# Combine weights from DRAM rows instead of a one-hot matmul, the output projection inside the expert loop, and half of the gating moved into it

## The reference, cut to what matters

```python
xn = _layernorm(x)                       # layer 0 before this: differential attention, MXFP4 ffn
s  = attn(xn) @ Wo + bo                  # 16 heads of 16
w, idx = _gate(xt, gate_w)               # top 4 of 16 experts, weights sum to 1
combine = einsum('tk,tke->te', w, one_hot(idx))
h1 = einsum('td,eid->tei', xt, W1); h3 = einsum('td,eid->tei', xt, W3)
g  = silu(h1) * h3 * combine[:, :, None]
y  = einsum('tei,edi->td', g, W2)
z  = silu(xt @ Ws1.T) * (xt @ Ws3.T) @ Ws2.T
x  = x + s * silu(y + z)
```

## Time and profile before

| | us |
|---|---|
| median of 3 runs | 946.36 |
| profiled execution, its own time | 948.34 |
| its span in the profile | 946.6 |
| start of `experts` (first instruction behind the barrier) | 672.5 |
| unit 2 begins on PE | 706.8 |
| last matmul of `down` ends | 933.9 |

### The profile page before, as it was taken

How to read it: one execution, slowest core, us unless ns; L and a number is a source line. 1 busy time by engine, 2 the same in 40 slices (tenths; PEclk the granted TensorE clock), 3 DMA queues, 4 the chain that set the end, 5 groups by cost and what they waited for, 6 DMA issues and landing times. The chain is left out here.

```text
span 946.6 us, 12914 instructions
## 1 busy us (share of the span) xinstructions
PE 791.8 (84%) x3682; PEld 386.6 (41%) x3682; DVE 508.8 (54%) x1448; ACT 424.5 (45%) x925; POOL 411.4 (43%) x753
## 2 busy tenths in 40 slices
PE   3848999889889998853695989788479999999995
PEld 2322333323323322223461223222257777777774
DVE  3748777767666765014428768672024444444445
ACT  2422555545545654511131457567314444444442
POOL 0831676425333242212221222342337677777774
PEclk9965999999999999955986799899779999999998
DMA  5485331100110110120076462232100000000001
GB/s 167 150 267 117 80 85 29 44 19 14 42 35 13 42 30 18 28 72 10 0 213 188 127 174 68 73 120 75 56 12 0 0 0 1 0 1 0 0 0 45
DMA packets 52206, 57.09 MB, mean 60 GB/s; under 512 B 13338, under 2 KB 39291, under 8 KB 52142
## 3 DMA queue, kind: packets, MB, share of 16 engines
q1 hardware_dynamic: 52148, 56.42, 21.3%
HBM read 34.70 MB, written 15.40 MB: 53 GB/s over the span
## 5 line engine op out<-in xcount | busy, mean ns | idle before, releaser
L660 ACT ACTIVATE top<-ps 128x512 f32<-128x512 f32 (+3 forms) x384 | 161.3, 497 | 156.5 <-PE ps L608 152.5
L591 PE MATMUL ps<-mid 96*128 96x512 bf16 (+3 forms) x576 | 192.3, 362 | 27.0 <-PEq L230 11.5
L608 PE MATMUL ps<-mid 99*128 99x512 bf16 (+3 forms) x576 | 182.4, 340 | 28.1 <-DMA mid<-top 9.5
L694 DVE CUSTOM_DVE_ANT_0 ps<-ps,keep 128x512 f32<-128x512 f32 (+3 forms) x384 | 183.9, 503 | 28.6 <-PE ps L591 27.4
L1374 PE MATMUL ps<-xp,wp 128*128 128x512 f32 (+1 forms) x600 | 146.9, 394 | 8.3 <-POOL wp L1467 8.3
L628 PE MATMUL ps<-top,mid 128*33 128x512 f32 (+3 forms) x768 | 150.5, 515 | 0.4 <-ACT top L660 0.4
L1374 PEld LDWEIGHTS ps<-xp,wp 128*128 128x128 f32 (+1 forms) x600 | 113.4, 189 | 34.1 <-issue 9.2
L777 POOL TENSOR_SCALAR_AFFINE_SELECT top<-top 128x128 f32<-128x128 f32 x256 | 72.4, 302 | 115.5 <-ACT top L660 110.7
L608 PEld LDWEIGHTS ps<-mid 99*128 99x128 bf16 x576 | 56.0, 100 | 152.6 <-issue 59.5
L698 DVE TENSOR_REDUCE top<-ps 128x1 f32<-128x512 f32 x128 | 88.0, 688 | 49.6 <-PE ps L591 49.6
L660 ACT ACTIVATE mid<-ps 128x512 f32<-128x512 f32 (+1 forms) x192 | 81.5, 493 | 62.2 <-PE ps L608 60.0
(11 more groups left out here) (201 smaller groups left out, 835.2 us busy)
## 6 DMA issues: line engine op xcount, KB each, us to landing
mid<-part_scratch SPq DMA_DIRECT2D x9, 1152.0 KB, 8.9
part_scratch<-top SPq DMA_DIRECT2D x18, 384.0 KB, 5.0
top<-in_w SPq DMA_DIRECT2D x16, 396.0 KB, 4.0
part_scratch<-top SPq DMA_DIRECT2D x18, 256.0 KB, 5.0
top<-inverse_scratch SPq DMA_DIRECT2D x16, 256.0 KB
mid<-part_scratch SPq DMA_DIRECT2D x9, 384.0 KB, 3.9
top<-in_w SPq DMA_DIRECT2D x8, 384.0 KB, 5.5
part_scratch<-top SPq DMA_DIRECT2D x18, 128.0 KB, 5.9
```

What stands on the lines that cost most here:

```text
L591: nc.tensor.matmul(ps[:, s_bank(turn), 0:w], queries(pair, m)[0:PARTS, i * P:(i + 1) * P], keys(pair, m)[0:PARTS, c * 512:c * 512 + w], st ...
L608: nc.tensor.matmul(ps[:, ST_BANK + n % AHEAD, 0:w], keys(pair, m)[0:STACK, j * P:(j + 1) * P], queries(pair, m)[0:STACK, q0:q0 + w], start ...
L660: nc.scalar.activation(pr[:, n % RING, 0:w], ps[:, ST_BANK + n % AHEAD, 0:w], ACT.Exp, scale=0.25).then_inc(p_ready, 1)
L694: ins = nc.vector.tensor_tensor_reduce(bank, bank, msk[:, 512 - w:512], -1.0 if low else 1.0, 3e38 if low else -3e38, ALU.add, ALU.min if ...
```

## The change

In `middle`, the combine weights stay float32: the split into three parts goes, PE transposes them in float32, ACT copies them to a tile `rows17`, and SP writes this to a DRAM tensor `combine_rows` (17 rows of 1024) at the stage's end. The first fetches of rows in layer 1 attention wait for that write.

In `experts`, the matmul L1382, its table and its bank go. For each unit SP issues two DMAs that read one 2 KB row each of `combine_rows` and repeat it over the partitions of that expert, into one of two tiles `cw`; `g` reads `cw` in place of PSUM. From unit 2 on, SP waits for `g` of two units before. The projection moves: token tiles 0 to 3 behind `down` of unit 3's step, tiles 4, 5 and 6, 7 in the steps of tiles 22 and 23 of the first half, into two banks, and DVE's additions of `bo` go to steps 3 and 24. PE's first matmuls wait only for the parts that they read. The first four tiles are transposed, gated and stored at the end of the loop (PE in the last two steps, ACT and DVE behind their last unit's work), and only tiles 4 to 7 behind `down`; the copy of `yT` is shared by ACT and DVE.

```diff
@@ middle, sync
+                sp.wait_ge(cT_ok, NC)
+                sp.dma_start(comb, rows17).then_inc(env["comb_kept"], 16)
@@ middle, scalar
-                    nc.scalar.copy(combT[:, c, :], psb[0:51, 2, c * 512:(c + 1) * 512]).then_inc(cT_ok, 1)
+                    nc.scalar.copy(rows17[:, c * 512:(c + 1) * 512], ps[0:E + 1, 2 + c, :]).then_inc(cT_ok, 1)
@@ middle, vector
-                        link(nc.vector.memset(cb[:, :, E:E + 1], 0.5))
-                        link(nc.vector.tensor_copy(cp[:, :, 0, :], cb[:, :, :]))
-                        link(nc.vector.tensor_tensor(cr[:, :, :], cb[:, :, :], cp[:, :, 0, :], ALU.subtract))
-                        link(nc.vector.tensor_copy(cp[:, :, 1, :], cr[:, :, :]))
-                        nc.vector.tensor_tensor(cp[:, :, 2, :], cr[:, :, :], cp[:, :, 1, :], ALU.subtract).then_inc(cb_ok, 1)
+                        nc.vector.memset(cb[:, :, E:E + 1], 0.5).then_inc(cb_ok, 1)
@@ experts, sync
+                def combine_weights(n):
+                    c, i = divmod(n, GI)
+                    if n >= 2:
+                        sp.wait_ge(g_ok, n - 1)
...
+                    for lo, hi in ((0, cut), (cut, r)):
+                        e = min((i * P + lo) // I, E)
+                        sp.dma_start(cw[lo:hi, n % 2, :], comb[e:e + 1, c * 512:(c + 1) * 512].to_broadcast([hi - lo, 512])
+                                     ).then_inc(cw_ok[n % 2], 16)
+                combine_weights(0)
+                combine_weights(1)
                 sp.dma_start(wo1[:, :, :], env["wo1"].rearrange("(c p) n -> p c n", p=P)).then_inc(ld, 16)
                 sp.dma_start(bo[:, :], env["bo"].partition_broadcast(P)).then_inc(ld, 16)
-                sp.dma_start(ones[:, :], env["onehot"]).then_inc(ld, 16)
                 env["last_inverses"](sp)
+                for n in range(2, UNITS):
+                    combine_weights(n)
@@ experts, tensor
+                            if begin and bank == H1 and j == 1:
+                                pe.wait_ge(xl_ok, 1)
+                            if begin and bank == H1 and j == 2:
+                                pe.wait_ge(wl_ok, 1)
...
-                    if isinstance(n, int) and n == 0:
-                        through_wo()
-                        pe.wait_ge(s1_ok, 4)
-                    nc.tensor.matmul(ps[0:r, CB + b, :], ones[:, bass.ds(i * P, r)], combT[:, c, :],
-                                     start=True, stop=True).then_inc(c_ok, 1)
...
+                    if c == 0 and isinstance(i, int) and 3 <= i < 4:
+                        for q in range(2):
+                            through_wo(q)
+                    if c == 0 and isinstance(i, int) and i >= GI - 3 and i < GI - 1:
+                        through_wo(2 + i - (GI - 3))
+                    if c == 1 and isinstance(i, int) and i >= GI - 2:
+                        if i == GI - 2:
+                            pe.wait_ge(s1_ok, 4)
+                        for t in range(2):
+                            back(2 * (i - (GI - 2)) + t, SB_ + i - (GI - 2), t * D)
@@ experts, vector
-                    dve.wait_ge(c_ok, n + 1)
+                    dve.wait_ge(cw_ok[b], cw_turn(c, k, i))
...
-                    nc.vector.tensor_tensor(g[0:r, b, :], a3[0:r, b, :], ps[0:r, CB + b, :],
-                                            ALU.mult).then_inc(g_ok, 1)
+                    nc.vector.tensor_tensor(g[0:r, b, :], a3[0:r, b, :], cw[0:r, b, :], ALU.mult).then_inc(g_ok, 1)
+                    if c == 0 and isinstance(i, int) and i in (3, GI - 1):
+                        for q in range(2):
+                            summed(q if i == 3 else 2 + q)
+                    if c == 1 and isinstance(i, int) and i == GI - 1:
+                        gates(0)
                 sweep(nc.vector.Fori, step)
+                gates(1)
+                dve.wait_ge(y_ok, UNITS)
+                nc.vector.tensor_copy(yT[:, 1, 1, :], ps[:, YB + 1, :]).then_inc(yTd_ok, 1)
```

More of the change, by code:

```diff
@@ L143, in program @@
         st6o = sb("st6o", [P, 4, 2, 6], F32, high)
[L144 to L145 removed]
+        comb = nc.dram_tensor("combine_rows", [E + 1, T], F32, kind="Internal").ap()
+        row_stats, comb_kept = sem("row_stats"), sem("comb_kept")
         v0 = sb("v0", [P, 4, NT, 33], F32, mid)
@@ L1297, in experts @@
         bo = new("bo_s", [P, D], F32)
-        ones = new("onehot_s", [51, NI], BF16)
+        cw = new("cw_s", [P, 2, 512], F32)
         s1 = new("s1", [P, NT, D], F32)
@@ L1327, in sweep, with tiles, pairs @@
                     step(c, i, i)
+        def tiles(q):
+            return slice(2 * q, 2 * q + 2)
+        def pairs(v):
+            return v.rearrange("p (t d) -> p t d", t=2)
         def slot(c, k):
@@ L1343, in _ @@
+                for q in range(2):
+                    sp.wait_ge(fo_ok, q + 1)
+                    sp.dma_start(out[2 * q * P:2 * (q + 1) * P, :].rearrange("(t p) d -> p t d", p=P),
+                                 gg[:, tiles(q), :]).then_inc(stored, 16)
+                for t in range(4, NT):
+                    sp.wait_ge(fo_ok, t - 1)
                     sp.dma_start(out[t * P:(t + 1) * P, :], gg[:, t, :]).then_inc(stored, 16)
-                sp.wait_ge(stored, 16 * NT)
+                sp.wait_ge(stored, 16 * (2 + 4))
@@ L1346, in _ @@
             @block.tensor
             def _(pe):
[L1349 to L1359, removed]
@@ L1361, in _, with through_wo @@
-                pe.wait_ge(xl_ok, 1)
+                def through_wo(q):
+                    if q == 0:
+                        pe.wait_ge(ld, 32)
+                        pe.wait_ge(env["combined1"], NC * 2)
+                    if q >= 2:
+                        pe.wait_ge(s1_ok, q - 1)
+                    for t in (2 * q, 2 * q + 1):
+                        for k in range(KD):
+                            last = nc.tensor.matmul(ps[:, SB_ + q % 2, (t % 2) * D:(t % 2 + 1) * D],
+                                                    o1[:, k, t * P:(t + 1) * P],
+                                                    wo1[:, k, :], start=k == 0, stop=k == KD - 1)
+                    last.then_inc(s_mm, 1)
@@ L1363, in hidden, with back @@
+                def back(t, bank, at):
+                    for k in range(KD):
+                        last = nc.tensor.transpose(ps[:, bank, at + k * P:at + (k + 1) * P],
+                                                   yT[:, t // 4, k, (t % 4) * P:(t % 4 + 1) * P], idf[:, :])
+                    last.then_inc(z_ok, 1)
                 def hidden(c, k, i):
                     n, b, r = c * GI + i, slot(c, k), rows(i)
+                    begin = isinstance(n, int) and n == 0
                     if isinstance(n, int) and n == GI:
@@ L1367, in hidden @@
                         pe.wait_ge(xl2_ok, 1)
-                    pe.wait_ge(wl_ok, n + 1)
+                    if begin:
+                        pe.wait_ge(xh_ok, 1)
+                        pe.wait_ge(wh_ok, 1)
+                    else:
+                        pe.wait_ge(wl_ok, n + 1)
                     if not (isinstance(n, int) and n < 2):
@@ L1409, in _ @@
                     down(NC - 1, i, i)
-                for t in range(NT):
-                    c = t // 4
-                    pe.wait_ge(yT_ok, c + 1)
-                    for k in range(KD):
-                        last = nc.tensor.transpose(ps[:, t, k * P:(k + 1) * P],
-                                                   yT[:, c, k, (t % 4) * P:(t % 4 + 1) * P], idf[:, :])
-                    last.then_inc(z_ok, 1)
+                pe.wait_ge(yT_ok, 2)
+                pe.wait_ge(yTd_ok, 1)
+                for t in range(4, NT):
+                    back(t, H1 + t - 4, 0)
             @block.scalar
             def _(act):
-                act.wait_ge(ld_m, 16 * 25)
                 def high_w13(b, i):
@@ L1431, in _, with gates @@
                 nc.scalar.copy(xp[:, 0, :, 512:T], xT[:, :, 512:T]).then_inc(xh_ok, 1)
+                def gates(q):
+                    act.wait_ge(z_ok, 2 * q + 2)
+                    nc.scalar.activation(ty[:, q, :], ps[:, SB_ + q, :], ACT.Tanh, scale=0.5).then_inc(ty_ok, 1)
                 def step(c, k, i):
@@ L1489, in _, with residual @@
                 sweep(nc.gpsimd.Fori, step)
-                for t in range(NT):
-                    pool.wait_ge(gated, t + 1)
-                    nc.gpsimd.tensor_tensor(gg[:, t, :], gg[:, t, :], xs[:, t, :], ALU.add).then_inc(fo_ok, 1)
+                def residual(part, done):
+                    pool.wait_ge(gg_ok, done)
+                    nc.gpsimd.tensor_tensor(gg[:, part, :], gg[:, part, :], xs[:, part, :], ALU.add).then_inc(fo_ok, 1)
+                for q in range(2):
+                    residual(tiles(q), 2 * q + 2)
+                for t in range(4, NT):
+                    residual(slice(t, t + 1), 4 + 2 * (t - 4) + 2)
             @block.vector
```

91 lines of the change are left out of this document (55 added, 36 removed).

## The result

The changed kernel takes 914.29 us (median of 4 runs, 911.00 to 916.78) and the kernel before 947.09 (4 runs, 945.02 to 949.48): ratio 0.9665, 95% interval 0.9637 to 0.9693, 32.8 us less. 914 was predicted. The profiled execution, which took 916.78 us, has a span of 915.0 us, against 946.6.

The account below looks back on a forecast made before the run. PE alone was taken to bound the `experts` loop. From the profiled 948.3 us, -26.2 - 14.9 + 3.0 + 7.1 + 0.9 - 2.5 + 0 = -32.6 gave 915.7, hence a median of 914; own range 909 to 918, 8 in 10 to 927.

Parts of the forecast that it names:

- the tail's first step: End of `experts`: the last `down` ends as late behind the last `hidden` as before, so no change.
- The loop, 4.63 to 4.08 a step: `experts` loop: without the one-hot matmul and its cost to neighbours, 48 steps save 26.2 us.
- POOL fits in 4.08: `experts` loop: POOL's longest closed chain with `g` is 4.01 us a step, so PE stays the bound.
- rival A: `experts` loop: step stays at 4.3 or more, 925 us, or 4.72 by POOL's chain, 945; chance 0.20, 0.02 near 945.
- Weights by DMA hidden: `experts` loop: `cw` is there about 4.4 us after `g` of n-2, needed after 7.5, so hidden.
- Start of the loop: Start of `experts`: reciprocals' write issued at 681.0, L481 done at 688.2, unit 2 at 691.9 instead of 706.8.
- Half clock at unit 2: Start of `experts`: unit 2, not the projection, now bears PE's half clock behind idle time, +3.0 us.
- Projection in the loop: `experts` loop: the projection's 32 matmuls and three changes of type now stand in the full loop, +7.1 us.
- the transposes ahead of the last `hidden`: End of the `experts` loop: four transposes at 0.22 us each, +0.9 us.
- The tail: Behind the last `down`: four tiles instead of eight, DVE's copy about 1.2 us after `down`; -2.5 us, bounds 0 and -4.3.
- `middle`: Stage `middle`: DVE operations go (-1.2), float32 transposes +0.7, DMA issue +0.5; sum 0, bounds -1.2 and +2.
- an earlier unit 2: Start of `experts`: unit 2 starts 14.9 us earlier, as unit 1 fills idle time and the projection moves behind.

Follow-up runs that it names:

- lead_one: The changed kernel with SP issuing a unit's combine weights when `g` of the unit before is done, not of two before; 931.54 us, one run.
- projection_first: The changed kernel with the output projection back behind unit 0, all else kept; 915.47 us, ratio 0.9660 to the kernel before.
- table_51_rows: The changed kernel with the old 51-row one-hot table load put back, unused, ahead of the reciprocals' write; 922.06 us, one run.
- pool_late: The changed kernel with POOL's last attention scaling behind its units 0 and 1, and the reciprocals sent earlier on SP; 904.96 us, ratio 0.9561 to the kernel before.
- g_from_psum: The changed kernel with `g` multiplying by a PSUM bank instead of the combine weights, which are fetched but left out; 911.17 us, one run.

## Why the prediction was right, step by step

The mechanisms came out as forecast; only the tail's first step went otherwise. That the median agrees to 0.3 us is luck in part: the terms were off by up to 1.1 us, and four executions of the changed kernel spread from 911.0 to 916.8.

- *The loop, 4.63 to 4.08 a step*: as predicted, to the hundredth, and for the reason given. 47 such steps lie between unit 2 and the last `hidden`, -25.8; the 48th lies in the tail.
- *POOL fits in 4.08*: yes. Its order let `g` in behind L1518 and held the W2 remainder back, so that POOL was busy 3.73 us a step and rival A's 4.72 did not come.
- *Weights by DMA hidden*: yes. lead_one shows 3.3 us from `g` to weights that can be used, where I had taken 4.4; the price was too high, on the safe side.
- *Start of the loop*: unit 2 at 693.0, I had said 691.9. The write went out at 680.8 (681.0) and L479 ended at 689.4, where I had 688.2: the read took 4.1 us to POOL's start and not 3.8, and it was issued at 684.1, not 683.2. -13.8 instead of -14.9. That the write stood behind the 51 rows is shown by the two runs with the table.
- *Half clock at unit 2*: +2.7 against its own 2.72 (+3.0).
- *Projection in the loop*: 3.45 + 1.73 + 1.73 = 6.9 (+7.1); the transposes ahead of the last `hidden` 0.44 (+0.9). At 0.11 us each they take half of the 0.22 that I read from the tail's row of 16. That row was one of half clock, and I took it for one of full. The window of the kernel before, over those transposes:

```profile
934.50:935.50 1.00, 1.00 (x7) 1.00 (x6) 0.29 (x1) 0.96 (x3) 0.00 (x0) 0.50 0.00 0
```

- *The tail*: -2.1 from the end of the last `hidden` (19.3 to 17.2) instead of -2.5. The mis-sized term: that `down` would end "as late behind the last `hidden` as before". It ended 1.6 us later: it began 0.3 later (5.21 us behind the last `hidden` instead of 4.89), as `g` took 1.07 us there instead of 0.68 beside POOL's W2 remainder, and took 1.26 more, by the clock, which it does only in some executions. All the rest of the tail is 3.7 shorter; the bound was 4.3. I put this to the gates' move into the loop, but no run takes that move back. DVE's copy began at once behind this late `down`, and I had put it 1.2 us behind; in projection_first, with `down` at full clock, it began 0.7 behind.
- *`middle`*: +0.1, I had said 0. From DVE's memset at the end of the routing to PE's first matmul of the next stage it is 3.91 us against 3.78.

The sum in the traces: -13.8 + 2.5 - 25.8 + 6.9 + 0.4 - 2.1 = -31.9, with 0.1 to 0.2 at the projection's borders; the spans differ by 31.6. (The 2.5 is 5.44 less the 2.95 that unit 2 took in the earlier trace rows.)

In one respect the text was right without separating two causes. It booked 14.9 us to an earlier unit 2 and took 3.0 and 7.1 back, net -4.8. Of the 14.9 it put 3.9 to the table that goes and didn't say what the move of the projection brings by itself; its figures leave -0.9. The runs divide it: projection_first shows the move at nothing that can be told, and table_51_rows the table at 5.2 us for unit 2 and 4.4 in the stage. So the net gain at the start is the table's, a load that the first part of the change removed by the way.

## What to carry to other kernels

A small transfer that others wait for must not stand behind a load whose rows divide over few DMA engines: 51 rows instead of 48 cost 3 us here. Where PE runs slow behind an idle stretch (0.50 behind 10.5 and 11.4 us here), moving work out of the stretch that pays it only changes who pays; closing the idle time (pool_late) was worth 9 us. Price a matmul of another type inside a run by the step with and without it, not by its own row: the row said 0.32 us, the step 0.55.

## What the runs showed that I had not expected

- Two traces of two kernels can mislead about the clock. The last `down` took 2.91 us behind 2.03 us of idle PE in the changed kernel and 1.66 behind 1.63 us in g_from_psum, as if 0.4 us of idle time had turned into 1.65 of delay. The same 2.03 us left it at full clock in four other kernels and 2.01 in a fifth. Whether 1.5 us of idle time is safe these traces don't show either: it held in two executions (1.53 before, 1.63 in g_from_psum).
- With seven matmuls of no use in that gap (0.46 us of idle time left) the clock held in both executions profiled. That they are what held it isn't shown, and they brought 0.1 us of the part behind the last `hidden`.
- A DVE product and a POOL product that both read SBUF lengthened each other (0.69 to 0.87 and 0.74 to 1.16 us) for 48 units, and it cost nothing in the loop, since PE bounded the step; the same 0.4 us delays the last `down` in the tail, where nothing covers it.
